# State-space layer and routed experts on one core: the experts' weights turned by DMA inside the blocks, kept in DRAM, and fetched into memory as it comes free

## What is computed

```python
# n = layernorm(x), over the 512 numbers of a token
s    = sigmoid(silu(n @ s_w1.T + s_b1) @ s_w2.T + s_b2)
u    = (n @ B_w.T + B_b) * s
h[t] = h[t-1] @ A.T + u[t]
y    = (h @ C_w.T + C_b + n @ D_w.T + D_b) * sigmoid(n @ g_w.T + g_b)
x    = x + y
...
# n = layernorm(x) again
chosen = argmax(n @ gate_w.T)
out    = x + n + expert_w[chosen] @ n
```

## Time and profile before

| | |
|---|---|
| median of 3 runs | 977.93 us (977.08 to 978.43) |
| the profiled execution | 977.28 us, span 975.5 us |
| PE busy | 937.7 us, 96% of the span |
| DVE, ACT, POOL busy | 674.4, 553.2 and 400.8 us |
| granted clock of PE | 0.984 over the span |
| DMA | 117.43 MB, mean 120 GB/s |

### The profile page before, as it was taken

The page is one execution under the profiler, slowest core; times in us unless marked ns, Lnnn a source line. Parts: engine busy times, 40 slices in busy tenths (PEclk is TensorE's granted clock), DMA queues, the critical chain, the costliest instruction groups (busy, mean ns, idle before and its releaser), DMA issues. The chain is left out here.

```text
span 975.5 us, 16231 instructions
## 1 busy us (share of the span) xinstructions
PE 937.7 (96%) x4769; PEld 767.8 (79%) x4770; DVE 674.4 (69%) x1655; ACT 553.2 (57%) x824; POOL 400.8 (41%) x522
## 2 busy tenths in 40 slices
PE   8999999999999999999999999999659999999995
PEld 7688888888888888888888888888557888888884
DVE  6677877868778787877868778777975444444442
ACT  5357465564746547465564746542565656666662
POOL 1040716436172552716436172551472333333332
PEclk9999999999999999999999999999879999999998
DMA  9623063351724416053251724412383554544441
GB/s 319 202 50 86 21 154 91 82 141 33 173 59 116 135 39 173 24 152 92 81 142 33 173 61 114 119 11 88 121 302 120 155 169 157 166 162 154 146 142 57
DMA packets 110685, 117.43 MB, mean 120 GB/s; under 512 B 69141, under 2 KB 69909, under 8 KB 110624
## 3 DMA queue, kind: packets, MB, share of 16 engines
q1 hardware_dynamic: 97040, 77.66, 30.5%
q0 software_dynamic: 10800, 33.70, 9.5%
q10 hardware_dynamic: 2784, 5.31, 1.6%
HBM read 64.85 MB, written 37.90 MB: 105 GB/s over the span
## 5 line engine op out<-in xcount | busy, mean ns | idle before, releaser
L509 POOL DMA_INDIRECT out<-gate,ids x71 | 69.9, 984 | 154.6 <-DVE gate L1105 116.0
L449 POOL TENSOR_SCALAR ln_var_eps<-ln_mean_var 128x4 f32<-128x4 f32 x16 | 3.6, 223 | 312.7 <-DVE ln_mean_var L838 312.7
L1105 DVE TENSOR_TENSOR gate<-y,x_rows 128x512 f32<-128x512 f32 x71 | 49.1, 691 | 108.2 <-PE y L1436 108.2
L1436 PE MATMUL y<-expert_hi,x1T_hi 128*128 x284 | 119.3, 420 | 2.2 <-DVE x1T_lo L1099 2.2
L1436 PE MATMUL y<-expert_hi,x1T_lo 128*128 x284 | 112.8, 397 | 0.0
L1436 PE MATMUL y<-expert_lo,x1T_hi 128*128 x284 | 112.3, 396 | 0.0
L1141 PE MATMUL gates<-GwT_hi,xT_hi 128*128 128x512 f32 x256 | 105.0, 410 | 0.0
L1141 PE MATMUL y<-DwT_hi,xT_hi 128*128 128x512 f32 x256 | 102.1, 399 | 0.5 <-DVE gateT L760 0.5
L595 ACT ACTIVATE joined<-flipped 128x1024 uint16<-128x1024 uint16 x60 | 82.2, 1370 | 34.3 <-DVE xT_lo L966 27.9
L1142 PE MATMUL gates<-GwT_lo,xT_hi 128*128 128x512 f32 x256 | 100.9, 394 | 0.0
L1143 PE MATMUL y<-DwT_hi,xT_lo 128*128 128x512 f32 x256 | 100.4, 392 | 0.0
(11 more groups left out here) (250 smaller groups left out, 2418.3 us busy)
## 6 DMA issues: line engine op xcount, KB each, us to landing
x_rows<-routed_rows SPq DMA_DIRECT2D x71, 258.0 KB, 2.6
x_in<-L_attn_x SPq DMA_DIRECT2D x32, 512.0 KB, 4.4
x_rows<-L_attn_x SPq DMA_DIRECT2D x32, 512.0 KB, 4.5
raw_weights<-L_ffn_expert_w ACTq DMA_DIRECT2D x5, 1024.0 KB, 7.2
raw_weights<-L_ffn_expert_w SPq DMA_DIRECT2D x3, 1024.0 KB, 6.7
routed_rows<-padrow SPq DMA_DIRECT2D x9, 258.0 KB
out<-gate,ids POOLq DMA_INDIRECT x71, 2.8
raw_weights<-L_attn_D_w SPq DMA_DIRECT2D x1, 1024.0 KB, 7.8
```

The lines of the kernel that those rows point to most:

```text
L509: nc.gpsimd.indirect_dma_start(out=out_rows, out_offset=bass.IndirectOffsetOnAxis(ap=ids[m][:, 0:1], axis=0), in_=res[m], in_offset=None, ...
L1105: nc.vector.tensor_tensor(res[m], Y[m % 2][:], rows[m][:, 0:D], ALU.add).then_inc(S_["slot_result"], 1)
L1436: ins = nc.tensor.matmul(Y[m % 2][:], x2T[a][:, k, m % 2 * P:(m % 2 + 1) * P], flat[w][:, bass.ds(first + k * D, D)], start=(k == 0 and a ...
```

## The change

The expert weights no longer pass through PE and no longer in the tail. Each block takes two of the 32 pieces (a piece is here 128 output rows of an expert, 128x512): SP loads a piece into `raw_weights`, ACT copies its 16-bit halves apart, a DMA transpose turns them, ACT joins them and rounds to the high part, DVE takes the low part, and SP stores both parts to a DRAM tensor `turned_experts`. In the last block and the tail, SP loads the eight experts, 2 MB each, from there into their place as the block stage's tensors under it come free; those tensors are laid out in a new order for this. The 48 first slots read a second register, `slot_need`, and wait until the first four experts, or all eight, are in.

```diff
+    turned_w = nc.dram_tensor("turned_experts", (E, P, 2 * KD * D), f32, kind="Internal").ap()
...
-            We = [later.enter_context(nc.sbuf_tensor("expert" + h, [P, E, KD, D], f32r)) for h in ("_hi", "_lo")]
+            We = later.enter_context(nc.sbuf_tensor("experts", [P, E, 2, KD, D], f32r))
...
+            def load_piece(b, j):
+                e, f = expert_piece(b, j)
+                wait(sp, w_halved[j], b)
+                sp.dma_start(w_raw[j], expert_w[e, f * P:(f + 1) * P, :]).then_inc(w_loaded[j], 16)
+            def flip_piece(b, j):
+                sp.wait_ge(w_halved[j], b + 1)
+                wait(sp, w_joined[j], b)
+                sp.dma_start_transpose(w_flipped[j], w_halves[j]).then_inc(w_flip[j], 16)
+            def store_piece(b, j):
+                e, f = expert_piece(b, j)
+                sp.wait_ge(w_low[j], b + 1)
+                sp.dma_start(turned_w[e].rearrange("p (h k d) -> p h k d", h=2, k=KD)[:, :, :, f * P:(f + 1) * P],
+                             w_parts[j].bitcast(f32)).then_inc(w_sent[j], 16)
+            def take_expert(e):
+                for j in range(2):
+                    sp.wait_ge(w_sent[j], 16 * 2 * (e + 1))
+                sp.dma_start(We[:, e].rearrange("p h k d -> p (h k d)").bitcast(f32), turned_w[e]).then_inc(S_["experts_in"], 16)
...
-            for e in range(RING):
-                load_expert(sp, e)
+            for j in range(2):
+                load_piece(0, j)
             for b in range(NBLK):
+                last = b == LASTB
+                if last:
+                    sp.wait_ge(S_["joined"], NT * LASTB)
+                    take_expert(0)
+                if b > 0:
+                    for j in range(2):
+                        flip_piece(b, j)
+                        if not last:
+                            load_piece(b + 1, j)
+                    store_piece(b - 1, 1)
+                if last:
+                    sp.wait_ge(S_["bt_psum"], NBLK)
+                    sp.wait_ge(S_["silu_lo"], KH * NBLK)
+                    take_expert(1)
+                    sp.wait_ge(S_["s2_psum"], NBLK)
+                    sp.wait_ge(S_["scan_lo"], NSTEP * LASTB + 1)
+                    sp.wait_ge(S_["xT_lo"], NT * NBLK)
+                    take_expert(2)
                 for n in range(NB):
...
+                    if b == 0 and n == 0:
+                        for j in range(2):
+                            flip_piece(0, j)
+                            load_piece(1, j)
...
+                store_piece(b, 0)
+            store_piece(LASTB, 1)
+            sp.wait_ge(S_["scoresT_psum"], 2 * LASTB)
+            sp.wait_ge(S_["down_psum"], NBLK)
+            take_expert(3)
+            sp.wait_ge(S_["experts_in"], 16 * E // 2)
+            sp.wait_ge(S_["g_psum"], NT * NBLK)
+            for e in range(4, 7):
+                take_expert(e)
+            sp.wait_ge(S_["h_lo"], NBLK)
+            sp.wait_ge(S_["g_sum"], NT * NBLK)
+            sp.wait_ge(S_["yb_ready"], NT * NBLK)
+            take_expert(7)
...
+                else:
+                    halve_piece(0, 0)
+                    halve_piece(0, 1)
+                join_piece(b, 0)
                 if ahead:
                     join(b + 1, 0)
...
-            experts(0, 3)
+            scatter(LASTB - 1, 0)
             rstd2(LASTB, 1)
-            scatter(LASTB - 1, 0)
-            experts(3, E_STEPS[4])
             scatter(LASTB, 1)
-            experts(E_STEPS[4], NE)
...
                 over(b, 4)
+                low_piece(b, 0)
                 if not ahead:
+                    low_piece(b, 1)
                     list_gaps()
...
+                if first == 0:
+                    then(nc.vector.tensor_scalar(slot_at[:, 0:n], slot_e[:, 0:n], float(E // 2), float(16 * E // 2), ALU.is_ge, ALU.mult))
+                    then(nc.vector.tensor_scalar(slot_need[:, 0:n], slot_at[:, 0:n], float(16 * E // 2), None, ALU.add))
...
+            def slot_product(s, m, early):
+                if early:
+                    counted_waits(pe, (S_["experts_in"], pe.value_load(slot_need[0:1, bass.ds(s, 1)], min_val=8 * E, max_val=16 * E)))
```

More of the change, by code:

```diff
@@ L670, in _ @@
                 body(b)
-            def experts(first, end):
-                for n in range(first, end):
-                    act.wait_ge(S_["expert_turned"], n + 1)
-                    nc.scalar.activation(We[0][:, n // KD, n % KD, :], EBANKS[n % NEB][:], ACT.Copy
-                                         ).then_inc(S_["expert_hi"], 1)
-                    if by_pool(n):
-                        nc.scalar.activation(We[1][:, n // KD, n % KD, :].bitcast(f32), EBANKS[n % NEB][:], ACT.Copy
-                                             ).then_inc(S_["expert_full"], 1)
-                    if n % KD == KD - 1 and n // KD + RING < E:
-                        load_expert(act, n // KD + RING)
-            experts(0, E_STEPS[0])
             for pair in range(2):
@@ L716, in _ @@
             slot_base(0, 0)
-            slot(0, 0, 0)
-            experts(E_STEPS[5], NE)
-            for s in range(1, M):
+            for s in range(M):
                 slot(s, s, 0)
@@ L1062, in _ @@
                 body(b, b % 2, b // 2)
-            def experts(first, end):
-                for n in filter(lambda n: not by_pool(n), range(first, end)):
-                    dve.wait_ge(S_["expert_hi"], n + 1)
-                    nc.vector.tensor_tensor(We[1][:, n // KD, n % KD, :], EBANKS[n % NEB][:],
-                                            We[0][:, n // KD, n % KD, :].bitcast(f32), ALU.subtract
-                                            ).then_inc(S_["expert_lo"], 1)
             y_biased(LASTB)
@@ L1111, in slot @@
                     slot_sum(s - 1, (m - 1) % M, turn - (m == 0))
-            experts(E_STEPS[2], E_STEPS[5])
-            slot(0, 0, 0)
-            experts(E_STEPS[5], NE)
-            for s in range(1, 2 * M):
+            for s in range(2 * M):
                 slot(s, s % M, s // M)
```

157 lines of the change are left out of this document (67 added, 90 removed).

## The result

The changed kernel takes 981.85 us (median of 12 runs, 979.23 to 982.97), the kernel before, on the same chip, 977.97 (12 runs, 977.06 to 979.86). The ratio is 1.0038, 95% interval 1.0029 to 1.0047: slower by 3.9 us, where the forecast was 979 and 1 us slower.

The account below looks back on a forecast made before the run. The prediction took PE to be the bound, busy throughout the blocks and losing time in the tail. Its sum, 977.3 + 5.3 (first block) + 0 (later blocks) - 10.5 (tail) + 7 (slots), gave 979.1, predicted as 979 us; range 966 to 986.

Parts of the forecast that it names:

- Block 0: First block: x's join on ACT starts at 51.4 instead of 46.12, behind the piece's work, and delays PE: +5.3 us.
- I take none: First block: no loss from PE's clock after its stop, since DVE splits the stop; up to 1.7 us more otherwise.
- Later blocks: Blocks after the first: ACT's near 6 us of added work falls into existing waits; costed at nothing, 3 us at most.
- Last block: Two low parts and two more slot-table steps put off the last scan step by 1.1 us, counted in the tail's term.
- Tail: From the last scan step to the first product: expert loads set the end, first product at 724.1 instead of 734.6, -10.5 us.
- the first slot's rows, issued far earlier, stand behind them: Tail, SP's queue: the rows wait behind the experts, landing at 721.1 where the last expert lands at 720.4.
- my 380 GB/s: Tail: the DMA rate taken for the last experts and scatters, giving 27.6 us of bytes.
- the rows don't wait: Tail: the queue serves loads side by side, rows are in time, first product at 714.5; 969.5 us in all, chance 0.13.
- Slots: First 48 slots: reading slot_need and two waits add 0.9 us against 0.6 slack over two slots; 0.15 a slot, +7 us.
- slots pay nothing: First 48 slots: the sequencer is far enough ahead to hide the reading; 972.1 us in all, chance 0.22.
- the sequencer pays more: First 48 slots, between turn and product: slack shrinks to 0.36, 0.27 a slot, 12.7 us; 984.8 in all, chance 0.2.
- the blocks lose their cover: Later blocks: the added work is not hidden, 0.3 us in each of 14; 983 us in all, chance 0.05.

Follow-up runs that it names:

- experiment 5: The changed kernel with ScalarE doing each piece's halving, join and high copy twice in blocks 1 to 15: 1016.8 us, ratio 1.0395.
- experiment 9: The changed kernel with block 14's scatter put back behind block 15's rstd2 on GpSimd: 983.16 us, ratio 1.0051.
- `slots_one_wait`: The changed kernel with one wait for all eight experts ahead of the slots, and no slot_need reading or wait inside them: 973.04 us, ratio 0.9937.
- `two_edits`: The changed kernel with one wait for all experts ahead of the slots and the first pieces' ScalarE work early in block 0: 966.19 us, ratio 0.9870.
- experiment 1: The same run as `slots_one_wait`: the changed kernel with one wait for all experts ahead of the slots and none inside them, 973.04 us.
- experiments 6 and 7: The changed kernel with the first four slots' rows issued ahead of experts 4 to 7 (987.69 us), or between experts 5 and 6 (986.1 us).

## Why the forecast came out as it did

*Block 0: right for the operand, wrong for the clock.* The chain named is the chain found, and 0.5 us small; the piece's transpose landed 0.8 us later than I had put. The stop did fall in two parts. But "I take none" for the clock, since the stop would be split, failed in the profiled execution: the half clock behind the second part took 1.6 us, close to the 1.7 that the prediction names as the most. It fell in some executions and not in others, so I can't say what the median has of it.

*Later blocks: right.* Nothing was lost in 14 blocks; they even gave back 1.5 us, which I had not seen and can't explain. That this cancels the 1.6 of the clock is luck. The working compared each operation with the wait at its place, and experiment 5 shows why that is the measure: with the same work again, 8.8 us a block still idle on ScalarE, a block grows by 2.3. The work ahead of `select` was doubled by 3.05 us, 1.08 were free there, and the 1.97 left come back as TensorE's 1.68; the rest of the 2.3 is the 0.58 at `scoresT`.

*Last block: right,* +1.0 us.

*Tail: right in size, wrong in its chain.* Moved by the 5.8 us of block 0, my last expert was to land at 726.2, the rows at 726.9 and the first product at 729.9. The last expert landed at 723.6 (its issue at 700.0 and 23.6 us, the longest of the eight below), the rows at 725.7, the first product came at 731.15.

```profile
DMA to landing us min/median/max: 8.0/12.1/23.6
```

The step that failed is "the first slot's rows, issued far earlier, stand behind them": they were issued at 717.5, because their buffers were still being read by scatter 14, and this landed 15.4 us after issue beside the experts. I had costed the scatters as bytes on the DMA, never as something that SyncE waits for. The number held because the bytes set the end on either path (experiment 9), and because two errors met: the experts were in 2.6 us earlier than put, since the DMA moved more than my 380 GB/s (432 from 710 to 720 us), and from the rows' landing to the first product it was 5.4 us instead of 3.0. That is luck, not knowledge of the path. The rows took 8.21 us with experts ahead and 2.56 without, as the order of the ring, which the prediction cites, would have it; but the scatter is on GpSimd's queue, not SyncE's, and its landing was held nevertheless. The same section of the Trainium skill (DMA: Bandwidth & Descriptors, Queues, rings and completion order) states this too, and I had not used it: the write that raises the semaphore lands only after every earlier write of its DMA engine, "across its queues". The 15.4, 12.5, 11.5 and 3 us of the runs fall with the bytes in flight, which agrees; whether it is this rule or the shared bandwidth alone, no run tells apart. The 5.4 us hold what my 3.0 left out: the turns at half clock (1.10 us where I had 0.60), slot 1's turn, which product 0 also follows, and the 0.84 us for the sequencer, which are gone in `slots_one_wait`.

*Rival "the rows don't wait":* shown wrong twice. They wait, 8.21 us behind the experts against 2.56, and when they are put ahead, the first product does come at 719.3, but the next rows pay.

*Slots: mis-sized by 1 us.* 0.15 a slot was worked out, 0.170 measured, 8.0 us instead of 7. I had priced the waits at 0.1 for the two and the reading at 0.8 of sequencer time, against a slack of 0.6, over two slots: 0.10 of a slot for the reading and 0.05 for the waits, where the runs give 0.090 and 0.080. The other 1.15 us is the start, 0.8 of it in the first slot. Its matmuls ran at half the clock, but so did part of them before the change (0.50 granted from 736 to 738 us), in 4.60 us; `slots_one_wait`, which starts as idle, has 4.60 too, `two_edits` 5.31. So this part varies and is not the price of the emptier tail as such. The rival "slots pay nothing" falls with experiment 1; "the sequencer pays more" had the direction, and its 0.27 a slot falls with the 0.170 of the trace.

*Rival "the blocks lose their cover":* its 0.3 us a block did not come, since the blocks got shorter.

So the forecast's +1.8 for the profiled executions and their +5.7 differ by three small misses of one sign: 0.5 in block 0, 1.2 ahead of the first product, 2.15 behind it. Beside them stand the two that cancel, the clock in block 0 and the shorter blocks. The saving of the tail is real, and block 0 and the slots' waits spend it and more.

## What to carry to other kernels

A gain of 10 us in a stage can be given away by two details elsewhere that cost nothing to avoid: work placed 11 us too late in one block, and a wait inside a loop for something that has long been there when the loop starts. Ask of each operation put beside other work what wait stands at exactly its place, not how idle its engine is: 6 us of work did not fit into 11.5 us of idle time. Ahead of a large load, list all that must pass the same DMA engines while it runs, on other queues too, and what each of these releases; putting one small transfer in front moves the stop to the next small transfer.

## What was not expected of the hardware

- The last part of a scatter (128 rows) on GpSimd's queue took 15.4 us to land beside 8 MB of loads on SyncE's, 12.5 beside 4 MB, 11.5 beside 8 MB when issued 11 us later, and about 3 with none in flight. So in these runs loads on one queue held back another's transfers, longer with more bytes, though not in proportion.
- The first slot's 12 matmuls took 5.36 us with TensorE at half the clock (1.2 GHz), after a stretch in which it was busy for 10.0 of 36.8 us; those of the next slot 2.80 (2.4 GHz). After a stop of 11 to 14 us in experiments 6 and 7 the next turn again took 1.1 us instead of 0.6. In block 0 a stop of 2.9 us was followed by half the clock in four profiled executions and by the full clock in one.
- A register read of 0.30 us costs a slot 0.090 or 0.049 us, according to what stands around it, and a wait against a register's value 0.080, long after the semaphore had passed it.
- The experts' loads of 2 MB, HBM to SBUF, moved 432 GB/s in one stretch of the changed kernel (710 to 720 us), above the 387 seen before the change. The Trainium skill (Perfetto Trace Analysis, Roofline) puts the 16 DMA engines of one core at about 435 GB/s, and the row agrees:

```profile
710.00:720.00 10.00, 1.83 (x15) 1.15 (x15) 3.13 (x13) 0.90 (x3) 2.68 (x3) 0.62 1.01 432
```
